# A spectral filter layer in float32: the small blocks' products as three products of rounded values and remainders, with one packing ring

## What is computed

```python
xf = jnp.fft.rfft2(x, axes=(1, 2), norm='ortho')   # 128 x 65 modes
xr, xi = real(xf), imag(xf)                        # in 8 blocks of 96 channels
o1r = relu(xr @ w1[0] - xi @ w1[1] + b1[0])
o1i = relu(xi @ w1[0] + xr @ w1[1] + b1[1])
o2r = o1r @ w2[0] - o1i @ w2[1] + b2[0]
o2i = o1i @ w2[0] + o1r @ w2[1] + b2[1]
o2  = softshrink(o2r, 0.01) + 1j * softshrink(o2i, 0.01)
out = jnp.fft.irfft2(o2, s=(128, 128), norm='ortho') + x
```

## Time and profile before

| | us |
|---|---|
| median of 3 runs | 5325.73 |
| lowest and highest | 5322.52, 5329.89 |
| the profiled execution's own time | 5328.54 |
| its span, first to last instruction | 5326.3 |
| TensorE busy | 5132.5 (96% of the span) |
| VectorE busy | 3851.1 (72%) |
| ScalarE busy | 2460.4 (46%) |
| GpSimd busy | 626.2 (12%) |
| mean granted TensorE clock | 0.997 of 2.4 GHz |

### The profile page before, as it was taken

How to read it: one execution, slowest core, us unless ns; L and a number is a source line. 1 busy time by engine, 2 the same in 40 slices (tenths; PEclk the granted TensorE clock), 3 DMA queues, 4 the chain that set the end, 5 groups by cost and what they waited for, 6 DMA issues and landing times.

```text
span 5326.3 us, 109469 instructions
## 1 busy us (share of the span) xinstructions
PE 5132.5 (96%) x42144; PEld 4070.8 (76%) x42144; DVE 3851.1 (72%) x5683; ACT 2460.4 (46%) x3569; POOL 626.2 (12%) x420
## 2 busy tenths in 40 slices
PE   6999999999999999999999999999999999999999
PEld 5777777778777787777777777777777777777776
DVE  5777777777777776777677777677776777767766
ACT  3444544445444454444444444444445444454443
POOL 0110011110111101111011110011100111101111
PEclk9999999999999999999999999999999999999999
DMA  3331333312333123331133321333212333123311
GB/s 104 96 89 29 84 97 96 101 30 71 97 96 101 44 57 97 96 101 49 52 97 96 101 68 42 88 96 101 77 42 78 96 101 93 40 65 96 100 49 48
DMA packets 1065699, 421.09 MB, mean 79 GB/s; under 512 B 1062816, under 2 KB 1062944, under 8 KB 1065120
## 3 DMA queue, kind: packets, MB, share of 16 engines
q1 hardware_dynamic: 1060384, 411.62, 29.2%
q10 hardware_dynamic: 4736, 1.60, 0.1%
HBM read 210.26 MB, written 201.33 MB: 77 GB/s over the span
## 4 chain that ended last, share of the span: by engine, by line
issue 88%; POOL 11%; POOLq 0%; DVE 0%
POOL x L874 11%; POOLq L873 0%; POOLq L877 0%; DVE x L822 0%; POOLq L874 0%; POOLq L886 0%
## 5 line engine op out<-in xcount | busy, mean ns | idle before, releaser
L874 POOL TENSOR_TENSOR x<-shrink_or_v,x 128x480 f32<-128x480 f32 (+1 forms) x416 | 626.0, 1505 | 4692.4 <-DVE shrink_or_v L815 4652.0
L787 DVE TENSOR_TENSOR shrink_or_v<-ps,wts 128x768 f32<-128x768 f32 (+1 forms) x544 | 502.0, 923 | 659.0 <-PE ps L529 632.3
L420 PE MATMUL ps<-tab,ring_a 128*64 128x128 f32 x6144 | 704.3, 277 | 38.0 <-DVE ring_a L736 25.8
L520 PE MATMUL ps<-wts,hbig 128*128 128x192 f32 x4160 | 734.7, 328 | 4.4
L420 PEld LDWEIGHTS ps<-tab,ring_a 128*64 128x64 f32 x6144 | 683.5, 139 | 54.2 <-DVE ring_a L736 29.2
L421 PE MATMUL ps<-tab,ring_a 128*63 128x128 f32 x6144 | 704.2, 277 | 0.0
L520 PEld LDWEIGHTS ps<-wts,hbig 128*128 128x128 f32 x4160 | 676.0, 190 | 32.7 <-issue 15.3
L433 PE MATMUL ps<-tab,ring_h 128*128 128x128 f32 x6144 | 694.6, 276 | 0.0
L433 PEld LDWEIGHTS ps<-tab,ring_h 128*128 128x128 f32 x6144 | 688.5, 192 | 5.5 <-DVE ring_h L845 5.5
L421 PEld LDWEIGHTS ps<-tab,ring_a 128*63 128x63 f32 x6144 | 683.4, 138 | 0.0
L615 ACT COPY ydg<-ps 127x512 f32<-127x512 f32 (+5 forms) x896 | 499.5, 567 | 382.7 <-PE ps L421 202.4
(11 more groups left out here) (62 smaller groups left out, 6864.7 us busy)
## 6 DMA issues: line engine op xcount, KB each, us to landing
x<-in_x SPq DMA_DIRECT2D x128, 1536.0 KB, 12.4
out<-x SPq DMA_DIRECT2D x352, 480.0 KB, 4.8
out<-x SPq DMA_DIRECT2D x32, 432.0 KB, 4.2
wts<-in_mix SPq DMA_DIRECT2D x16, 513.0 KB, 3.6
out<-x SPq DMA_DIRECT2D x32, 240.0 KB, 4.4
out<-x SPq DMA_DIRECT2D x32, 192.0 KB, 4.2
ydg<-row ACTq DMA_DIRECT2D x32, 48.0 KB
yedge<-row ACTq DMA_DIRECT2D x32, 0.8 KB
```

Source lines behind the costliest of these rows:

```text
L420: pe.matmul(o[0:HALF], slot[:, 0:HALF], mat("fwd_w"), start=True, stop=True)
L520: mm = pe.matmul(o, hbig[:, k * H:(k + 1) * H], mix_part("w2_big"), start=first, stop=False, skip_group_check=True)
L787: dve.tensor_tensor(parts(v), d, b2, ALU.add).then_inc(bias_done, 1)
L874: pool.tensor_tensor(xs[p][:, a:b, :], ucopy[g % 4][:, 0:b - a, :], mirror(xs[p], a, b), ALU.add).then_inc(plus_ready, 1)
```

## The change

1. `zsmall` gives way to `zsmall_hi` (cast on ScalarE, same place as the copy) and `zsmall_lo` (a subtraction on VectorE that reads PSUM, behind `zlo`'s). `w1hi` and `w1lo` grow from 128 to 384 columns. L487 and L502 become three FP32R products each. `zsmall_ready` is now given by VectorE's subtraction.
2. One ring of 5 slots takes the place of the two rings of 4. ScalarE's first packs of an item move from the mixing to the end of the inverse lines before it, and are five; five early and tail packs of the inverse lines are made instead of four.
3. VectorE's forward lines, edge copies and first two remainders of an item are moved behind the rows of the item before, in the loop's body, so that the loop's branch falls between the second remainder and the first fold.
4. The forward products of unit 1 write banks 4 to 7 where unit 0's and unit 1's shared bank 0, with other waits.
5. An image is loaded in eight transfers, outermost rows first from both ends, with a semaphore for each of four pieces; a fold waits for its pieces only. The doubling of the edge rows moves from the first fold to the last.

```diff
-RING_A = 4
-RING_H = 4
+RING = 5
 def packer_a(g):
-    return "act" if g < RING_A + 2 or g % 3 == 2 else "dve"
+    return "act" if g < RING + 2 or g % 3 == 2 else "dve"
-PACK_IN = {6: (0, 1), 7: (2, 3)}
...
         def z_bank(u, what):
-            return {0: Z_BANK, 1: OUT_BANK, "small": OUT_BANK + 1}[what] if u == 0 else Z_BANK
+            if u < 2 and what != 0:
+                return OUT_BANK + 2 * u + (what == "small")
+            return Z_BANK
...
-                    for i in range(LOADS):
-                        rows = slice(i * H // LOADS, (i + 1) * H // LOADS)
-                        sp.dma_start(xs[p][:, rows, :], src[:, rows, :]).then_inc(x_loaded[p], 16)
+                    for i in range(PIECES):
+                        a, e = i * LOAD_ROWS, (i + 1) * LOAD_ROWS
+                        for lo, hi in ((a, e + (e == HALF)), (H + 1 - e, H + 1 - max(a, 1))):
+                            sp.dma_start(xs[p][:, lo:hi, :], src[:, lo:hi, :]).then_inc(x_loaded[p][i], 16)
...
                 def fwd_big(q, u, h):
-                    if u:
-                        pe.wait_ge(zbig_ready, NP * q + part_at(u, h) - 1)
+                    if h == 0 and u in (1, 2):
+                        pe.wait_ge(zbig_ready, NP * q + part_at(u - 1, 0))
+                    elif h == 0 and u > 2:
                         pe.wait_ge(zsmall_ready, NU * q + u)
+                    elif u > 1:
+                        pe.wait_ge(zbig_ready, NP * q + part_at(u, 0))
...
                 def fwd_small(q, u):
-                    if u:
+                    if u > 1:
                         pe.wait_ge(zbig_ready, NP * q + last_part(u))
...
-                    pe.matmul(ps[0:r, SMALL_BANK, 0:n], mix_part("w1_small_small")[0:r, 0:r], zsmall[u % 2][0:r, 0:n],
-                              start=True, stop=False)
+                    pe.matmul(o, lo, zh, start=True, stop=False)
+                    pe.matmul(o, hi, zh, start=False, stop=False)
+                    pe.matmul(o, hi, zl, start=False, stop=False)
...
                 def mix1_rows(q, u):
+                    for w, z, stop in ((lo, zh, False), (hi, zh, False), (hi, zl, True)):
+                        for i in range(halves(u)):
+                            half = slice(i * SMALL, (i + 1) * SMALL)
+                            mm = pe.matmul(ps[:, BIG_BANK + i, 0:n], w[half], z[half, 0:n], start=False, stop=stop)
...
                 def remainder(q, u):
                     dve.wait_ge(zhi_ready, NU * q + u + 1)
                     dve.tensor_tensor(zlo[:, 0:n], zbig[u % 2][:, 0:n], zhi[:, 0:n], ALU.subtract).then_inc(zlo_ready, 1)
+                    dve.wait_ge(zsmall_hi_ready, NU * q + u + 1)
+                    dve.tensor_tensor(zsmall_lo[u % 2][0:r, 0:n], ps[0:r, z_bank(u, "small"), 0:n],
+                                      zsmall_hi[u % 2][0:r, 0:n], ALU.subtract).then_inc(zsmall_ready, 1)
...
 ScalarE's step, behind lines(q, p, 1):
+                            act.wait_ge(line_done, lines_before(q + 1, 0, 0))
+                            for g in range(RING):
+                                pack_lines(q + 1, 1 - p, g)
...
 VectorE's step:
+                def to_mixing(q, t, p):
+                    lines(q, p, 0)
+                    copy_edges(q)
+                    if p == 0:
+                        split_weights(t)
+                    remainder(q, 0)
+                    remainder(q, 1)
...
                     for p in range(PAIRS):
                         q = t * PAIRS + p
-                        lines(q, p, 0)
-                        copy_edges(q)
+                        if fold_next:
+                            fold_in(q, t, p, 1)
+                        for it in range(2, NU + 2):
...
+                        if fold_next:
+                            to_mixing(q + 1, t + p, 1 - p)
```

More of the change, by code:

```diff
@@ L206, in build @@
         edge = sb("edge", [128, 2, 2 * CB])
-        ring_a = [sb(f"ring_a{j}", [W, CG, 128]) for j in range(RING_A)]
-        ring_h = [sb(f"ring_h{j}", [128, CG, 128]) for j in range(RING_H)]
+        ring = [sb(f"ring{j}", [128, CG, 128]) for j in range(RING)]
         ps = ctx.enter_context(nc.psum_tensor("ps", [128, 8, 512], F32))
@@ L697, in step @@
                                 relu(q, it - 1)
-                            if it in PACK_IN and not (last and p == PAIRS - 1):
-                                act.wait_ge(pairs_folded, FOLDS * (q + 2))
-                                for g in PACK_IN[it]:
-                                    pack_lines(q + 1, 1 - p, g)
                         early_pack(q, 1)
@@ L711, in step @@
                         lines(q, p, 1)
+                        if not (last and p == PAIRS - 1):
+                            act.wait_ge(pairs_folded, FOLDS * (q + 2))
+                            act.wait_ge(line_done, lines_before(q + 1, 0, 0))
+                            for g in range(RING):
+                                pack_lines(q + 1, 1 - p, g)
                 act.wait_ge(cleared, 1)
                 act.wait_ge(pairs_folded, FOLDS)
-                for g in range(RING_A):
+                for g in range(RING):
                     pack_lines(0, 0, g)
@@ L822, in subtract, with wait_loaded, fold_in @@
                     dve.tensor_tensor(xm, ucopy[g % 4][:, 0:b - a, :], xm, ALU.subtract).then_inc(y_ready, 1)
+                def wait_loaded(p, times, i):
+                    a, b = fold_rows(i)
+                    for piece in range(a // LOAD_ROWS, (b - 1) // LOAD_ROWS + 1):
+                        dve.wait_ge(x_loaded[p][piece], times * 32)
+                def fold_in(q, t, p, it):
+                    for i in FOLD_IN[it]:
+                        wait_loaded(1 - p, t + 1 + p, i)
+                        fold(q + 1, 1 - p, i)
+                def to_mixing(q, t, p):
[5 more added lines that the diff above has]
+                    remainder(q, 1)
                 def step(t, last):
```

109 lines of the change are left out of this document (60 added, 49 removed).

## The result

The changed kernel takes 5174.17 us in the median of 4 runs (5172.48 to 5175.51), the kernel before beside it 5324.12 (5322.47 to 5329.89). The ratio is 0.9716, with a 95% interval of 0.9699 to 0.9733: 2.8% faster. The forecast was 5200 with a range of 5160 to 5265. The time lies in the range, but nearer to the rival in which the branch costs nothing in its new place (5168).

The account below looks back on a forecast made before the run. TensorE, busy 96% of the span, was taken to bound the kernel, through work and waits. 5326.3 - 90 - 14 - 45 + 27 + 5 - 9 = 5200 us, the median about the same; range 5160 to 5265.

Parts of the forecast that it names:

- small products and start of the mixing: Mixing on TensorE: FP32R small products and separate banks for the first forward products win 2.8 us an item, 90 us.
- fifth slot and packs in the rows: Forward lines: one more slot packed ahead removes TensorE's wait for ScalarE's packing, 0.45 us an item, 14 us won.
- branch gone from the lines: Forward lines of 14 items: VectorE's loop branch no longer delays them, 3.24 us each, 45 us won.
- branch in the mixing: Before the folds: VectorE's 3.57 us idle makes TensorE wait 1.9 in 14 items, 27 us lost, plus 5 for clock.
- loads in pieces: Start of the run: outer folds begin before the whole image is loaded, 9 us won once.
- change of shape: Small products in 64-row halves: 0.11 us on top of three paired FP32R products, together 0.80.
- subtraction out of PSUM: VectorE's new small remainder of 512 columns: 0.68 us, with bounds of 0.61 and 0.69.
- The wait in unit 0: Start of the mixing: TensorE waits 1.9 us for VectorE's new subtraction, where it had waited 1.4.
- third rival: VectorE late in every unit from new remainders, or wider waits at the mixing's start lowering the clock: 5244 us, chance 0.12.
- second rival: VectorE's loop branch costs nothing between the second remainder and the first fold: 5168 us, chance 0.13.

Follow-up runs that it names:

- the padded run: Changed kernel with a ring of four slots instead of five and 32 tiny memsets ahead of VectorE's loop: 5186.99 us, ratio 0.9742.
- the old banks: Changed kernel with unit 1's second part and small rows back in bank 0 and the earlier waits of its forward products: 5256.47 us, ratio 0.987.
- The run with the moved wait: Changed kernel with TensorE's wait for VectorE's small remainder placed behind a unit's six big products (unit 9 unchanged): 5141.98 us, ratio 0.9651.
- the run with one fill: Changed kernel with one tiny memset ahead of VectorE's loop: 5190.33 us, ratio 0.9746.
- 64 fills: Kernel before with 64 tiny memsets ahead of VectorE's loop: 5309.52 us in a single execution.
- One-row stores: Kernel before with each store carrying only the first row of its stretch, most output unwritten: 5299.11 us in a single execution.

## Why the prediction was right, and the step that failed

| step | predicted | measured | from |
|---|---|---|---|
| small products and start of the mixing | -90 | -91 | 32 x (97.76 - 94.91) |
| fifth slot and packs in the rows | -14 | -16 | 32 x 0.51; 13.9 by the padded run |
| branch gone from the lines | -45 | -43 | 14 x (25.76 - 22.18 - 0.51) |
| branch in the mixing | +27, +5 | +2 | 14 x (95.06 - 94.91) |
| loads in pieces | -9 | -8 | 37.86 to 29.17, and 0.34 longer lines in item 0 |

Together -156, the 156.1 of the spans.

**Small products.** L507 to L509 were predicted at 0.69 and take 0.68, and L526 was predicted at 0.80 and takes 0.80; the change of shape of 0.11, read off L502, holds for FP32R. The subtraction out of PSUM takes 0.68 (1342.91), as taken from the copy. The total of 2.85 an item was predicted as 2.8. The runs tell its makeup: with the new banks and float32 products the mixing is 1.60 shorter (97.76 to 96.16), and the FP32R products add 1.25, a gross gain of 2.6 less the 1.4 that their new wait costs. So the banks, with their waits, hold more of the net gain than the products, which the prediction, with one sum for both, did not say.

**The wait in unit 0.** Predicted as 1.9, from 1.8 to 3.7 behind the start of `fwd_small(0)`; it is 1343.65 less 1341.98, 1.67, from 2.0 to 3.7 behind that start (1339.97). The clock, which my third rival had falling behind it, fell in none of 32 items; behind 2.6 (the old banks) it fell in 21.

**The slot and the loads** were right within 3 us.

**The branch** is the step that failed, in its size. "The same 3.57 now falls between the second remainder and the folds": it was 1.64 to 1.94. The rest of that working holds: with 3.57 VectorE would have been 1.9 late, with the 1.63 less of item 8 it is 0.3 late, and TensorE's wait at 1361.09 is 0.24. I took the idle time in the old place as the price of the branch in every place. It is what is left of a fetch of 2.9 us or more, and that depends on three things: how long before the last operation's end the branch is taken (0.47 or 1.25 us in the traces of the two kernels), the data traffic beside it, and where its target lies in the program. The run with the moved wait, in which VectorE's program is the same and its gap a microsecond longer, shows the second, and the run with one fill the third. This one term is 30 us too high (+32 for +2); the others are each within 2 us and cancel. The time lay in the range because the range had been drawn for a branch that costs from nothing to 3.6. With the right price the sum is 5168 to 5170, that of the second rival, to which I gave 0.13. That was luck for the rival: its ground, that TensorE's branch shows no hole, was not the reason, for VectorE's branch does leave a hole in its new place, and the slack covers it.

**Left open.** Why the fetch packet starts 1.9 to 2.0 us behind the branch in the kernel before, and only 1.4 to 1.64 in the two programs that have the branch in the same place with the same traffic (64 fills; the changed kernel with the branch back). One-row stores and fills were not tried together. Nor was a fill count tried at which the changed kernel's 0.16 goes, nor the old banks with a loosened wait.

## What to carry to other kernels

A taken branch on VectorE was a fetch here, with 2.9 us or more from the branch to the next operation: put it where the engine has slack, behind operations that wait for nobody, so that part of it lies under them, and away from heavy transfers, and look behind it for a second idle time that the trace puts down to "issue", which padding ahead of the loop can move away. When a wait is moved or added, look at its length in one piece and at the clock behind it. By the idle time that the rows give, 1.5 us at the start of the mixing cost no clock in 32 items, and behind 2.6 us the clock fell in 21 of 32. The length doesn't decide it alone: behind the kernel before's waits for VectorE's packing the clock fell in two items with 1.67 and 1.68 us, and stayed in six with 1.60 to 1.76. And give a wait to the one instruction that needs it: moving it behind six products, with one fold moved away from the branch, was worth 47 us more than the change itself had.

## What the runs showed of the hardware that I had not expected

- One tiny instruction ahead of VectorE's loop makes the kernel 16 us slower, through 14 idle times of 1.17 to 1.46 us; 64 of them make the kernel before some 17 us faster.
- FP32R products of 64 rows pair up even when the three of one half stand ahead of the three of the other: six in 0.80 us both ways.
- The idle time behind a branch on VectorE ran from 1.64 us (DMA share 0.04) to 3.7 us (0.57), the same program on either side. Counted from the branch itself it was 2.9 to 4.95 us, since the branch is taken up to 1.25 us before the last operation ends.
- The clock's falls turn a wait's price: a wait of 2.6 us took 1.6 more in the items in which the clock went to 1.2 GHz behind it.
